# The head and the tail of the time mix in a modulated RWKV and expert layer: rows of modulation, the last O, the last X

## The reference

```python
mod = (silu(c) @ wmod).reshape(4, 6, 1, 512)
sa, ca, ga, sb, cb, gb = mod[:, 0], ..., mod[:, 5]
ga, gb = sign(ga) * max(abs(ga), 0.25), the same for gb
h = layernorm(x) * (1 + ca) + sa
x = x + ga * block(h)
h = layernorm(x) * (1 + cb) + sb
x = x + gb * experts(h)          # 2 shared and 16 routed experts, top 2

def block(x):
    h = layernorm(x, g1, b1); hh = shift by one token
    k, v, r = (h * m + hh * (1 - m)) @ W.T     # for Wk, Wv, Wr
    x = x + sigmoid(r) * wkv(k, v) @ Wo.T
    h = layernorm(x, g2, b2); hh = shift
    kk = (h * cm_mk + hh * (1 - cm_mk)) @ Wkey.T
    sr = sigmoid((h * cm_mr + hh * (1 - cm_mr)) @ Wcr.T)
    return x + sr * (silu(kk) @ Wval.T)
```

## Time and profile before

| | |
|---|---|
| median of 3 runs | 1078.58 us (1078.02 to 1079.64) |
| the profiled execution | 1081.21 us, its span 1079.5 us |
| granted TensorE clock, mean | 0.926 |
| TensorE busy | 912.0 us, 84% of the span |
| VectorE, GpSimd, ScalarE busy | 520.1, 404.7, 380.3 us |

### The profile page before, as it was taken

How to read it: one execution, slowest core, us unless ns; L and a number is a source line. 1 busy time by engine, 2 the same in 40 slices (tenths; PEclk the granted TensorE clock), 3 DMA queues, 4 the chain that set the end, 5 groups by cost and what they waited for, 6 DMA issues and landing times.

```text
span 1079.5 us, 13473 instructions
## 1 busy us (share of the span) xinstructions
PE 912.0 (84%) x4238; PEld 729.5 (68%) x4239; DVE 520.1 (48%) x877; ACT 380.3 (35%) x623; POOL 404.7 (37%) x311
## 2 busy tenths in 40 slices
PE   3788879999959997999999989999887499999800
PEld 0166668787847886788888778888666487877600
DVE  2598998985653111431351153137644344443366
ACT  1256464665534331222322123344312133333222
POOL 3042200100105454005015001855556989891074
PEclk8788989999978998899999999999999799999955
DMA  6625124122334358139226933646796688784377
GB/s 226 243 80 156 60 87 156 69 92 65 118 118 164 109 166 243 49 130 280 77 98 210 277 112 106 212 134 212 235 345 216 225 251 264 255 263 142 126 234 232
DMA packets 118369, 184.54 MB, mean 171 GB/s; under 512 B 10392, under 2 KB 55448, under 8 KB 117552
## 3 DMA queue, kind: packets, MB, share of 16 engines
q1 hardware_dynamic: 107856, 148.25, 41.4%
q0 software_dynamic: 10464, 35.66, 10.7%
HBM read 108.06 MB, written 75.81 MB: 170 GB/s over the span
## 4 chain that ended last, share of the span: by engine, by line
PE 61%; DVE 13%; DMA 7%; issue 6%; SPq 5%; POOL 4%; ACT 4%; POOLq 0%; DVEq 0%; ACTq 0%
PE kk_ps L374 4%; PE kk_ps L375 4%; PE kk_ps L376 4%; PE kv_ps L376 4%; PE kv_ps L374 4%; PE kv_ps L375 4%; SPq L503 4%; PE mm_ps L374 4%; PE mm_ps L375 4%; PE mm_ps L376 4%; PE up_ps L374 4%; PE dn_ps L374 3%; PE up_ps L375 3%; PE up_ps L376 3%; PE dn_ps L376 2%
## 5 line engine op out<-in xcount | busy, mean ns | idle before, releaser
L1443 DVE TENSOR_TENSOR silu<-kk_ps,silu 128x512 fp32r<-128x512 f32 x64 | 44.3, 692 | 255.7 <-ACT silu L1952 255.7
L374 PE MATMUL kk_ps<-xk,cm_w 128*128 128x512 f32 x256 | 104.7, 409 | 14.0 <-DVE xk L1484 10.5
L1948 ACT ACTIVATE kk_ps<-kk_ps 128x512 f32<-128x512 f32 x64 | 37.2, 582 | 193.2 <-PE kk_ps L376 193.2
L375 PE MATMUL kk_ps<-xk,cm_w 128*128 128x512 f32 x256 | 102.6, 401 | 0.0
L376 PE MATMUL kk_ps<-xk,cm_w 128*128 128x512 f32 x256 | 102.0, 398 | 0.0
L376 PE MATMUL kv_ps<-cm_w,silu 128*128 128x512 f32 x256 | 99.7, 389 | 0.0
L375 PE MATMUL kv_ps<-cm_w,silu 128*128 128x512 f32 x256 | 99.6, 389 | 0.0
L374 PE MATMUL kv_ps<-cm_w,silu 128*128 128x512 f32 x256 | 99.6, 389 | 0.0
L2143 POOL TENSOR_TENSOR rs<-mv,neghalf 128x1 f32<-128x1 f32 x16 | 16.0, 1001 | 171.0 <-DVE mv L1465 171.0
L2102 POOL TENSOR_TENSOR rs<-mv,neghalf 128x4 f32<-128x4 f32 x12 | 13.6, 1135 | 175.0 <-DVE mv L1172 174.9
L1728 DVE TENSOR_TENSOR xsT<-xs_ps,xsT 128x512 fp32r<-128x512 f32 x42 | 29.1, 692 | 89.3 <-ACT xsT L2029 89.3
(11 more groups left out here) (213 smaller groups left out, 2349.0 us busy)
## 6 DMA issues: line engine op xcount, KB each, us to landing
xs_s<-zero SPq DMA_DIRECT2D x52, 256.0 KB, 3.7
stage<-in_wex POOLq DMA_DIRECT2D x26, 512.0 KB
xsb<-xs_s SPq DMA_DIRECT2D x44, 256.0 KB, 3.4
ys_s<-ysb SPq DMA_DIRECT2D x41, 256.0 KB, 2.9
stage<-in_wcm SPq DMA_DIRECT2D x16, 512.0 KB, 3.8
wmod<-in_wmod SPq DMA_DIRECT2D x6, 1024.0 KB, 8.8
stage<-in_wtm SPq DMA_DIRECT2D x10, 512.0 KB, 4.2
ys_s<-zero SPq DMA_DIRECT2D x20, 256.0 KB, 3.7
```

What stands on the lines that cost most here:

```text
L374: pe.matmul(out, lhs[0], rhs[0], start=first, stop=False)
L375: pe.matmul(out, lhs[0], rhs[1], start=False, stop=False)
L1443: dve.tensor_tensor(silu[:, g % NSILU, 1, :], kk_ps[g % 2][:, :], silu[:, g % NSILU, 0, :].bitcast(F32), ALU.subtract).then_inc(s_silo, 1)
L1948: act.activation(kk_ps[g % 2][:, :], kk_ps[g % 2][:, :], ACT.Silu).then_inc(s_silu, 1)
```

## The change

- **Order of the rows.** wmod rows are loaded as 1, 0, 2, 5, 3, 4, without a wait, ahead of them only c; vecs and wrt go behind the first weights. TensorE first makes rows 1 and 0 of batch 0 as broadcasts into the two `raw_ps` banks (`first_rows`: the stationary side is one column of `cT`, repeated 128 times), then rows 0, 1, 2 and 5 into `mm_ps`, then the turns. Rows 3 and 4 are made between V tiles of batch 0 in the `tp_ps` banks.
- **Use.** ScalarE copies the broadcast row 1, plus 1, to `ca_bc`; VectorE reads the broadcast row 0 from its bank. ScalarE, not VectorE, copies all rows to `modr` (`rows_out`). VectorE floors row 2 ahead of the first differences and row 5 behind the last `wkv` of batch 0 (`gate_floor`, four operations). Rows 2 to 5 are stored when row 4 and both floors are there, behind halves 4 to 7 and the load of x of batch 1, ahead of the h0 stores of batch 1 and halves 8, 9. Rows 0 and 1 are stored behind the h0 of batch 0, for batch 1's broadcasts.
- **Order in the head.** The turns of the first two blocks go by token tile; differences are taken two, one and one; GpSimd makes rs2 between its first two weights; weights over `wmod` wait for the products.
- **Last S of batch 2.** In the last batch only tile 0 of S(2) stays ahead of O(3); tiles 1 to 3 go behind it, and their sigmoids and stores with them. `order1` and `bank_free` count by tile.
- **Last X and first xk.** X(3) is written to `hn`'s four tiles. xk of batch 0 goes through `xkr` and `raw`, four buffers, in one go; its low part is made by VectorE. The last four `sr_out` are behind it. The last norm is turned by token tile, its differences are taken two, one and one.

The core of the diff:

```diff
+        order1 = []
         for b in range(NB):
+            order1 += [(s, b, j) for s in "KVR" for j in range(4)]
+            if b == NB - 1:
+                order1.append(("S", b - 1, 0))
+            elif b:
+                order1 += [("S", b - 1, j) for j in range(4)]
+            order1 += [("O", b, j) for j in range(4)]
+        order1 += [("S", NB - 2, j) for j in range(1, 4)] + [("S", NB - 1, j) for j in range(4)]
...
@@ SP @@
-            sp.wait_ge(s_modsb, 2)
-            for i in (0, 1):
-                sp.dma_start(mod_s[i], modr[:, i]).then_inc(s_modst, 16)
-            load_bc(0)
-            for i in range(2, 6):
+            sp.dma_start(vecs[:, :, :], vecs_d).then_inc(s_bc, 16)
+            sp.dma_start(wrt[:, :, :], wrt_d).then_inc(s_bc, 16)
+            for i in row_order[2:]:
                 sp.dma_start(wmod[:, i], wmod_d[i]).then_inc(s_wmod[i], 16)
...
             store_h0(0)
+            sp.wait_ge(s_modsb, 3)
+            for i in (0, 1):
+                sp.dma_start(mod_s[i], modr[:, i]).then_inc(s_modst, 16)
             load_bc(1)
             load_x(1)
-            sp.wait_ge(s_modsb, 6)
+            for n in (4, 5, 6, 7):
+                load_tm(n)
+            sp.wait_ge(s_modsb, 7)
+            sp.wait_ge(s_ke, 3)
             for i in range(2, 6):
                 sp.dma_start(mod_s[i], modr[:, i]).then_inc(s_modst, 16)
-            sp.wait_ge(s_modps, 6)
-            for n in (4, 5, 6, 7):
-                load_tm(n)
...
             load_half(12, cm_half(12))
+            store_sr(NB - 2, [1])
             load_half(13, cm_half(13))
...
-            load_xk(0, [0, 1])
+            load_xk(0)
+            store_sr(NB - 2, [2, 3])
             store_xk(NB - 1)
-            load_xk(0, [2, 3])
             store_sr(NB - 1, [0, 1])
@@ TensorE @@
+            def first_rows(i):
+                pe.wait_ge(s_wmod[i], 16)
+                for k in range(KT):
+                    mm = pe.matmul(raw_ps[i][:, :], cT[:, k, 0:1].to_broadcast([P, P]), wmod[:, i, k, :],
                                    start=k == 0, stop=k == KT - 1)
                 mm.then_inc(s_modps, 1)
+            first_rows(1)
+            first_rows(0)
+            for i in range(3):
+                modulation(i, mm_ps[i])
+            modulation(5, mm_ps[3])
+            turn_by_tile(1, 0, [0, 1])
             turn(1, 0, [2, 3])
...
-            turn(2, NB - 1)
+            tokens_out("S", NB - 2, [1, 2, 3])
+            turn_by_tile(2, NB - 1, [0, 1])
+            turn(2, NB - 1, [2, 3])
             tokens_out("S", NB - 1)
@@ VectorE @@
+            def gate_floor(i):
+                src = modr[:, i]
+                dve.wait_ge(s_modsb, row_count(i))
+                done(dve.tensor_scalar(modt[:, 0], src, 0.0, 2.0, ALU.is_ge, ALU.mult))
+                done(dve.tensor_scalar(modt[:, 1], src, -1.0, 0.25, ALU.mult, ALU.max))
+                done(dve.tensor_tensor(modt[:, 1], src, modt[:, 1], ALU.max))
+                dve.scalar_tensor_tensor(out=src, in0=modt[:, 0], scalar=-1.0, in1=modt[:, 1],
+                                         op0=ALU.add, op1=ALU.mult).then_inc(s_ke, 1)
...
+                if b == 0:
+                    gate_floor(5)
...
+            xk_lo(0, range(KT))
@@ ScalarE @@
+            sr_out(NB - 2, [1])
             hn_out(2, NB - 1)
-            to_hT(2, NB - 1)
+            sr_out(NB - 2, [2])
+            to_hT(2, NB - 1, [0, 1])
+            sr_out(NB - 2, [3])
+            to_hT(2, NB - 1, [2, 3])
...
-            xk_hi(0, [0, 1])
-            sr_out(NB - 1, [0, 1])
-            xk_hi(0, [2, 3])
-            sr_out(NB - 1, [2, 3])
+            xk_hi(0)
+            sr_out(NB - 1)
```

More of the change, by code:

```diff
@@ L832, in _, with modulation @@
         def _(pe):
-            def modulation(i):
+            def modulation(i, bank):
                 pe.wait_ge(s_wmod[i], 16)
                 for k in range(KT):
-                    mm = pe.matmul(mm_ps[i % 4][0:NB, :], cT[:, k, :], wmod[:, i, k, :],
+                    mm = pe.matmul(bank[0:NB, :], cT[:, k, :], wmod[:, i, k, :], start=k == 0, stop=k == KT - 1)
+                mm.then_inc(s_modps, 1)
+            def first_rows(i):
+                pe.wait_ge(s_wmod[i], 16)
+                for k in range(KT):
+                    mm = pe.matmul(raw_ps[i][:, :], cT[:, k, 0:1].to_broadcast([P, P]), wmod[:, i, k, :],
                                    start=k == 0, stop=k == KT - 1)
@@ L848, in turn, with turn_by_tile @@
                     mm.then_inc(s_tp, 1)
+            def turn_by_tile(kind, b, blocks):
+                for k in blocks:
+                    if turned(kind, b, k) > 2:
+                        pe.wait_ge(s_hT, turned(kind, b, k) - 2)
+                for j in range(TT):
+                    pe.wait_ge(s_hn, hn_count(kind, b, j))
+                    for k in blocks:
+                        mm = pe.transpose(tp_ps[k % 2][:, j, :], hn[:, j, k * P:(k + 1) * P], ident[:, :])
+                        if j == TT - 1:
+                            mm.then_inc(s_tp, 1)
             def channels_out(s, b, tiles=range(KT)):
@@ L911, in _ @@
                     turn(2, b - 1, [0, 1])
+                else:
+                    pe.wait_ge(s_hT, turned(1, 0, KT - 1))
+                    modulation(3, tp_ps[0][:, :, :].rearrange("p j c -> p (j c)"))
                 channels_out("V", b, [2])
@@ L1311, in _ @@
             first_norm_d(0)
-            modulation(2)
             centred(1, 0)
-            modulation(3)
-            differences(1, 0)
+            dve.wait_ge(s_bc, 32)
+            dve.tensor_scalar(floor[:, :], vecs[:, V_FIRST, :], -1.0, PP0, ALU.mult, ALU.add).then_inc(s_ke, 1)
+            gate_floor(2)
+            differences(1, 0, [0, 1])
             mixed("K", 0, 0)
             mixed("K", 0, 1)
+            differences(1, 0, [2])
             mixed_lo("K", 0, 0)
-            modulation(4)
-            modulation(5)
             mixed("K", 0, 2)
+            differences(1, 0, [3])
             mixed_lo("K", 0, 1)
@@ L1859, in sr_out, with rows_out @@
                     act.activation(srb[:, t % 2], mm_ps[j][:, :], ACT.Sigmoid).then_inc(s_sr, 1)
+            def rows_out(i, bank):
+                act.wait_ge(s_modps, rows_summed(i))
+                if i in (1, 4):
+                    ins = act.activation(modr[:, i], bank[0:NB, :], ACT.Identity, bias=1.0)
+                else:
+                    ins = act.activation(modr[:, i], bank[0:NB, :], ACT.Copy)
+                ins.then_inc(s_modsb, 1)
+            act.wait_ge(s_modps, 1)
+            act.activation(ca_bc[:, :], raw_ps[1][:, :], ACT.Identity, bias=1.0).then_inc(s_modsb, 1)
             weight_hi(0)
             weight_hi(1)
+            for i in range(3):
+                rows_out(i, mm_ps[i])
             hn_out(1, 0)
+            rows_out(5, mm_ps[3])
+            act.wait_ge(s_bc, 32)
             to_hT(1, 0)
@@ L1916, in _ @@
                     to_hT(1, b + 1, [2, 3])
-                if b:
+                if b and more:
                     sr_out(b - 1, [1])
```

139 lines of the change are left out of this document (63 added, 76 removed).

## The result

The changed kernel takes 1047.62 us in the median of four runs (1046.09 to 1048.25), the kernel before 1078.3 beside it: a ratio of 0.9712 (95% interval 0.9695 to 0.9729). Forecast was 1048.7. The profiled execution took 1048.25, its span 1046.5, with a mean granted clock of 0.946 where it was 0.926.

The account below looks back on a forecast made before the run. TensorE, busy 84% of 1079.5 us, was taken as the bound, so only its waits count. Head 19.1 (22.4 less 3.3) plus tail 10.8 gave 29.9 off 1081.21: 1051.3 profiled, 1048.7 as median; range 1042 to 1062.

Parts of the forecast that it names:

- Products and the first pass: Head: six modulation products end at 29.6; VectorE's first pass meets GpSimd, whose 2.4 us the products hide.
- K, V, R: First batch on TensorE: third K mix 23.5 earlier, V ends at 67.3, R ends 23 to 24 earlier.
- the moved products cost nothing: Products 3 and 4, 7.0 us inside V, only fill R's former pause of 3.47 and its slow start.
- The hold: Row 5's floor, slowed beside `weight_lo`, delays its store: `rw_hi(0,0)` 4.3 late, then 3.3 late; bounds 0 to 6.
- weights 8 and 9 come 3 to 4 late ... No cost.: Loads queued behind SP's wait for the floor come 3 to 4 late relative to VectorE, costing nothing.
- Tail: Last O to third key: S tiles fill the norm wait (6.1), xk lies ready; 10.8 earlier, bounds 6.1 to 12.2.
- move as a whole: Later stages, bound by TensorE or chains starting with them, shift by the gain of head plus tail, 29.9.
- A: Rival: the floor slips between the two `weight_lo`, so no hold; 1045.4, chance 0.17.
- B: Rival: the tail gives its first term alone, as xk stays late; 1053.4, chance 0.11.
- C: Rival: modulation rows land late, row 5's product ends at 34.9, 5.3 lost; 1054.0, chance 0.11.
- D: Rival: TensorE's pause before K drops the clock to half through batch 0's K, V, R, O; +38, 1087, chance 0.05.
- E: Rival: the change doesn't do what it says, new waits take all back; about 1078, chance 0.03.

Follow-up runs that it names:

- e8: e7 with row 5's floor moved behind `rw_lo(0, 1)`, thus behind both `weight_lo`; 1040.54 us.
- e6: The changed kernel with weight halves 8 and 9 loaded ahead of SP's wait for the floor, the hold at rw kept; 1048.13 us.
- e3: The changed kernel with the first xk back in two buffers, in pairs, low part on GpSimd; 1051.87 us.
- e4: e3 with the last X also put back into `raw`; 1053.00 us.
- e10: The changed kernel run and profiled once more, nothing altered; 1047.04 us.
- e1: The changed kernel's head alone, with the whole tail put back as before the change; 1061.67 us.
- e7: The changed kernel with modulation rows laid in other buffers, so `rw_hi` waits for no store, and weight halves 8 and 9 loaded early; 1044.86 us.

## Why the prediction was right, point by point

**Products and the first pass.** Right: six products end at 30.0 (forecast 29.6). The sixteen records with 128 stationary columns took 0.4 more than those with 4 before (9.73 against 9.33, both with the slow start), inside the 0 to 0.8 bound. GpSimd cost more than reckoned: `nm`, 128 by 4, took 2.28 beside the second `weight_lo`, which I had put behind it, so hn starts at 27.5 and not 26.7, and the third K mix is 0.5 late. The rest of GpSimd's 2.4 was hidden by the products, as forecast.

**K, V, R.** The third K mix came 23.0 earlier for 23.5 forecast. V ended at 69.9 and not 67.3. The fourth low part came 23.9 earlier for 24.6, and 0.6 was lost at 50.4; the half rate of K until 42.4 is no loss against the forecast, as K ran so until 66.5 before. The rest was not followed. R ends 21.7 earlier for 23 to 24. In the change this cost nothing, as the turns behind R are done at 81.6 and ScalarE stands at its wait for the store until 81.84. Without that hold it does: in e8 hT waits 1.36 for the turns. So "the moved products cost nothing" is right beside the hold alone, and too narrow besides: they gain 6 by not standing ahead in ScalarE's order.

**The hold.** Forecast was that `rw_hi` comes 4.3 behind its order and hT 3.3. Measured: a wait of 3.37; the order is 22.0 earlier (weights 6 and 7), `rw_hi` 18.5 and hT 19.6, thus 3.5 and 2.4 behind it. The place was right and the size too high by 0.9, and not through what I took. I charged the floor by `wkv`'s 2.81 and thought operations with one SBUF input free. The two `TENSOR_SCALAR` were the held ones (2.63, 2.50), and those with two inputs ran behind them at 0.68. The Trainium skill's rule that I weighed and did not use (GPSIMD Engine Reference, 1. Specifications: two-port modes contend too) agrees with the trace, if the one-input `TENSOR_SCALAR` runs in such a mode. The Trainium skill's page SBUF — State Buffer (🔬 SBUF: two separate sides) says further that the pair of ports is held for the whole instruction and the other engine blocks until then; 2.63 + 2.50 over GpSimd's 5.16 agrees. The extra 1 us that I gave this rule did not come: each `weight_lo` held one operation, and the two others, behind both, took their 0.68.

**The step that failed: "weights 8 and 9 come 3 to 4 late ... No cost."** SP's wait stands ahead of their load. They were issued at 84.86, 12.0 earlier than before (96.81) where the order of ScalarE is 22.0 earlier: 10 late, not 3 to 4. ScalarE waited 5.23 for them, and the 19.6 of hT became 17.0 at K of batch 1. e6 takes that wait away and K is 2.6 earlier, which is the 19.6 again. I had seen the wait in SP's order and left it unpriced: the eight transfers between the stores and these loads, and the landing (8.4 us from issue to the start of `weight_hi`, with the load of x right behind) were not worked out.

**Tail.** 11.1 for 10.8. The first term 6.1 is 6.0 in the trace; S(3) 7.8 for 7.6; of the remaining 3.3 the xk in four buffers are 2.4 (e3), and the other 0.9 was not taken apart. (The third key of before starts at 344.03 in the trace and not at 344.25, so the forecast should have had 10.6.) One term fell: X was to end earlier for its four buffers, by 1.9 of waits. It kept its 6.28, GpSimd's (e4).

**Later stages "move as a whole".** In e10 they do (27.5 and 27.6), in the first profile not (28.5 and 33.0), and the medians lie between. Not settled.

**Rivals.** A (no hold) is out by 3.37, B by the keys, C by the gapless products, D by the clock, back at full at 42. (D was priced too high: it took the lengths 0.63 and 0.39, but the starts are 0.43 and 0.23 apart, 0.2 a matmul and not 0.24.) E is out by the time.

**The size.** 28.5 at the keys from 1078.58 would be 1050.1; forecast had 29.9. The median was 1047.62, and in e10, whose keys give 1051.1, 1047.04: 2.5 and 4 below what the landmarks say. So part of the closeness of 1048.7 is luck: the keys 1.4 too high (head 2.1 at K), a remainder of 2.5 to 4 in the other direction. In nine of twelve rows of the table the ratio, times 1078.6, gives 1.4 to 3.6 us more than the keys, in e1, e3 and e4 1.1 to 3.4 less; each interval is about 4 wide on either side. What the remainder is, is open.

## What to carry to other kernels

When a wait is put into a queue, list every transfer behind it and work out its landing against its first reader: taking the two loads out from behind SP's wait gave 2.6 at K of batch 1, taking the priced hold away gave 1.3 as long as they stood there. A matrix product that uses idle TensorE time may still cost nearly its full length (6.0 of 7.0 here) through the copy that empties its bank, if this stands ahead of work on ScalarE's critical order. And a landmark is only worth what a second profile of the same program says: 0.1 at K of batch 1, 1.0 at the keys. The 1.4 between e7 and e8 is of that size and lies in a tile where the clock differed.

## What the runs showed of the hardware

A 4 by 512 `TENSOR_SCALAR` took 0.41 alone and 2.63 beside a GpSimd subtraction of 2.58; a 128 by 4 operation with two inputs took 0.15 alone and 2.28 beside one. In both cases the small operation ended with the other's end or one short operation behind it, whatever its own size. And TensorE's return from the half level (0.43 between matmuls) to the full (0.23) came at 134.7 in one profile of the change and at 136.7 in the other, with the stage started within 0.2 of each other: 1.0 us of one V tile. An edit that starts a stage 2.6 earlier lost half of this within it (e6), where the return did not come earlier with the work.
